# Two heads' values in one set of PSUM rows, value products divided by key tile, and last experts' sums by TensorE, in a four-layer decoder kernel

## The chip, the cores and the metric

The kernel runs on one core of one Trainium2 chip. The metric is the device time of one execution in microseconds (us). TensorE is called PE here, VectorE DVE, ScalarE ACT, GpSimd POOL and SyncE SP. Each runs its own queue of instructions in order, and they wait for one another by semaphores.

## The reference

The input x has 16 sequences of 256 tokens with 128 values each, and a context of 16 x 64 x 64. Four layers each do a self attention, a cross attention and a feed-forward part (dense or chosen experts), each added to x and layer-normalised. What matters for the change:

```python
# self attentions of layers 0 to 2, 16 heads of 8 values, 256 queries x 256 keys
scores = einsum('bhqd,bhkd->bhqk', q, k) * 8 ** -0.5     # + mask or bias
out    = einsum('bhqk,bhkd->bhqd', softmax(scores, -1), v)
# L0 self: rotary.  L0 cross: causal self attention + cross attention, added.
# L1 self: bias by distance, out * sigmoid(x @ Wgate.T + bgate).
# L2 self: additive mask, repeated three times, out of one is q of the next.
# L2 feed-forward: causal rotary attention, then capped experts.
# L3 feed-forward: each token's four chosen experts of 16
y = sum over 4 chosen of w[k] * expert_k(x);  x = layernorm(x + y)
```

## The kernel before

Everything but the experts' rows stays in SBUF. Stages follow one another; each of the later attentions begins its first slots inside the last slots of the stage ahead (`lead`).

`SelfAttention` is built five times: s0 (L0, rotary), s1 (L0 causal with cross attention), s3 (L1, bias and gate), s6 (L2, three repetitions), s8 (the attention of L2's feed-forward part, kind "keep"). A unit is one sequence (and one repetition): 16 units in each, 48 in s6, 112 in all. The work is written out by hand in slots: unit u starts 8 slots (10 in s1) after unit u-1, and in slot g every engine's `..._slot` issues what the offsets call for. In the first 8 slots of a unit PE makes plain scores of two heads a slot (L1314, with masks L1348) and DVE takes their maxima (L1359, L1362); at slot 8 `dve_neg_max` (L670) splits the negated maxima into two bf16 terms, with four instructions. From slot LE = 12 on PE makes transposed scores with the maxima subtracted (L1452), and ACT takes exponentials into PT (L1412, in s3 L1403 after DVE has added the bias at L1480).

Four times in a unit (j = 0 to 3, slots LE+3, 5, 7, 9) `pe_pv` (L1489) multiplies four heads' exponentials by their values: 9 columns a head (8 values and a one, whose product is the sum), each head in its own 32 PSUM rows of bank 6, all four at once. j = 0 and 1 fill the bank. ACT copies it to TV (`act_tv`, L718), PE transposes it with four fp32 transposes (`pe_tvt`, L727), and DVE takes reciprocals of the sums (L738) and multiplies twice (L744). j = 2 and 3 do all of this again. s1 has a third round for its cross attention (L754, L759). Then come the transpose of the unit's output (`pe_oot`, L767), the output projection (L348), residual, norm and the transpose for the next stage, at `OUT` and `TURN`. Reciprocal square roots of the norms are made by `newton` (L492), twelve small instructions on POOL.

The values of a chunk (two sequences) are projected by `pe_values` (L1263) and put in one of three buffers VA by ACT or DVE (L1277, L1285); for chunk 0 that is 13 to 19 slots before its first unit. PSUM bank 7 is shared in turn by all transposes and projections (`pj_take`).

The last stage, s12 (`ChosenExperts`, "marked"), runs blocks of expert rows. POOL scatters each block's results (`pool_result`, L3751), gathers the results of chunks 0 to 4 (`pool_gather`, L3763), and makes the root of the chunk before in between. The results of chunks 5 to 7 come by plain DMA, and `dve_results` (L3797) sums them on DVE (L3804, L3807), takes moments and normalises.

## Time and profile before

| | us |
|---|---|
| time, median of 3 runs | 4086.99 (4083.13 to 4093.6) |
| the profiled execution's own time | 4104.95 |
| its span | 4103.1 |
| granted PE clock, mean | 0.87 |
| PE busy | 3225.7 (79%) |
| DVE busy | 2729.5 (67%) |
| ACT busy | 2072.7 (51%) |
| POOL busy | 1254.2 (31%) |

A row of the groups has the line, engine, operation and tiles, the count, busy us and the mean ns of one, then idle time ahead of it. Stretches are given in us from the span's start. The five attentions lie at about 50 to 355 (s0), 373 to 760 (s1), 986 to 1374 (s3), 1869 to 2610 (s6) and 2807 to 3070 (s8); s12's blocks end at 4060.

### The profile page before, as it was taken

Reading aid. Unit: us, or ns where it says so; the run is one execution under the profiler, and the core shown is the slowest. Engines: PE = TensorE matmul, PEld = TensorE weight load, DVE = VectorE, ACT = ScalarE, POOL = GpSimd, SP = SyncE. Lnnn points to the kernel's source line nnn. Section 1 sums busy time; section 2 is a strip of 40 time slices with the busy share of each in tenths; the row PEclk is TensorE's granted clock in tenths of the full one; section 3 lists DMA queues with packets and bytes.
Section 4 is the critical chain, followed back from the end, with each engine's and each line's share of the span. In section 5 each row is a group of like instructions: output and inputs, shape, how many; then the busy total and the mean of one; then the engine's idle time right before and its main releaser. Section 6 shows DMA issues by size and latency. Waiting matters only on the chain.

```text
span 4103.1 us, 91932 instructions
## 1 busy us (share of the span) xinstructions
PE 3225.7 (79%) x33262; PEld 2229.8 (54%) x33262; DVE 2729.5 (67%) x7583; ACT 2072.7 (51%) x4651; POOL 1254.2 (31%) x2347
## 2 busy tenths in 40 slices
PE   6886888696888676967898989677883579879884
PEld 2443555473556455854555555344553456669884
DVE  5884767364778576547787878476766468865455
ACT  2664656322444453535787878453660234345563
POOL 2321222102121234451111111243322424534666
PEclk9987999697999787977999999687995599989997
DMA  5423332032221322231212121423412260122323
GB/s 92 69 38 55 59 54 39 21 100 40 37 39 18 57 60 66 85 72 38 47 30 45 29 43 31 59 39 60 60 32 71 72 112 21 50 85 85 94 75 92
DMA packets 322828, 232.76 MB, mean 57 GB/s; under 512 B 53901, under 2 KB 305531, under 8 KB 322199
## 3 DMA queue, kind: packets, MB, share of 16 engines
q1 hardware_dynamic: 308106, 198.55, 24.7%
q0 software_dynamic: 13408, 27.54, 2.2%
q8 instruction: 269, 4.41, 0.5%
q14 instruction: 181, 1.48, 0.1%
q10 hardware_dynamic: 864, 0.79, 0.1%
HBM read 69.28 MB, written 55.75 MB: 30 GB/s over the span
## 4 chain that ended last, share of the span: by engine, by line
PE 26%; DVE 13%; POOL 7%; issue 6%; ACT 4%; DMA 2%; SPq 1%; DVEq 0%; ACTq 0%; POOLq 0%
PE ps L1505 4%; PE ps L1314 3%; PE ps L3939 2%; PE ps L3948 2%; PE ps L1348 2%; POOL PT L3763 2%; PE ps L727 2%; PE ps L1452 2%; ACT PT L1412 1%; DVE M L1362 1%; POOL L_sorted_results L3751 1%; PE ps L1126 1%; DVE X L406 1%; DMA SKB<-MT 1%; DVE BS L378 1%
## 5 line engine op out<-in xcount | busy, mean ns | idle before, releaser
L1412 ACT ACTIVATE PT<-ps 128x512 f32<-128x512 f32 (+1 forms) x1600 | 812.0, 560 | 339.6 <-PE ps L1348 247.4
L1362 DVE TENSOR_REDUCE M<-ps 128x2 f32<-128x512 f32 x1024 | 652.6, 683 | 128.6 <-PE ps L1348 103.8
L1314 PE MATMUL ps<-SKB 51*128 51x256 bf16 (+3 forms) x3584 | 414.4, 276 | 115.7 <-DVE M L1362 66.2
L1359 DVE TENSOR_REDUCE M<-ps 128x3 f32<-128x384 f32 x768 | 390.6, 550 | 150.5 <-PE ps L1348 92.7
L1505 PE MATMUL ps<-PT,VA 128*9 128x256 f32 (+1 forms) x7168 | 455.7, 374 | 1.4 <-ACT PT L1412 1.2
L4021 ACT ACTIVATE SKB<-ps,SKB 128x128 f32<-128x128 f32 x1032 | 295.1, 370 | 242.4 <-PE ps L3939 241.0
L1452 PE MATMUL ps<-SKB 53*128 53x256 bf16 (+3 forms) x3584 | 357.8, 268 | 47.2 <-DMA SKB<-MT 37.3
L1348 PE MATMUL ps<-tri,idh 64*128 64x128 bf16 x5120 | 392.9, 222 | 0.0
L4091 DVE COPY SKB<-SKB 128x1028 f32 (+1 forms) x258 | 185.7, 720 | 259.7 <-PE ps L3948 232.4
L1314 PEld LDWEIGHTS ps<-SKB 51*128 51x128 bf16 (+1 forms) x3584 | 131.2, 96 | 385.9 <-DVE M L1362 158.1
L3948 PE MATMUL ps<-SKB 128*128 128x128 f32 x2064 | 286.6, 284 | 28.4 <-ACT SKB L4021 28.3
L649 POOL TENSOR_TENSOR FF<-FF,HH 128x512 f32<-128x512 f32 (+1 forms) x118 | 128.9, 1092 | 546.4 <-ACT HH L638 546.3
L1348 PEld LDWEIGHTS ps<-tri,idh 64*128 64x128 bf16 x5120 | 278.2, 98 | 28.0
L3939 PE MATMUL ps<-SKB 128*128 128x128 f32 x2064 | 290.7, 286 | 0.0
L3948 PEld LDWEIGHTS ps<-SKB 128*128 128x128 f32 x2064 | 263.4, 200 | 31.5 <-ACT SKB L4021 31.3
L3939 PEld LDWEIGHTS ps<-SKB 128*128 128x128 f32 x2064 | 267.5, 202 | 0.5 <-issue 0.3
L496 POOL TENSOR_TENSOR NW<-NW 128x4 f32<-128x4 f32 x336 | 70.6, 210 | 600.7 <-DVE NW L489 546.6
L1505 PEld LDWEIGHTS ps<-PT,VA 128*9 128x9 f32 x7168 | 156.4, 92 | 168.4 <-issue 40.1
L727 PE MATMUL ps<-idf,TV 128*128 128x128 f32 x1088 | 183.6, 294 | 51.6 <-ACT TV L718 17.8
L1452 PEld LDWEIGHTS ps<-SKB 53*128 53x128 bf16 (+1 forms) x3584 | 160.1, 97 | 84.5 <-DMA SKB<-MT 41.4
L3821 POOL DMA_INDIRECT L_sorted_rows<-XT,GG x144 | 145.7, 1012 | 188.8 <-DVE SKB L4098 79.1
L1403 ACT ACTIVATE PT<-ps 128x768 f32<-128x768 f32 x128 | 103.9, 811 | 185.9 <-DVE ps L1480 185.9
(520 smaller groups left out, 6403.3 us busy)
## 6 DMA issues: line engine op xcount, KB each, us to landing
SKB<-HH SPq DMA_DIRECT2D x1212, 64.0 KB
SKB<-HH SPq DMA_DIRECT2D x576, 32.0 KB
L_sorted_results<-SKB SPq DMA_DIRECT2D x195, 64.0 KB
PT<-L_sorted_rows SPq DMA_DIRECT2D x150, 64.0 KB
SKB<-in_L3f_w SPq DMA_DIRECT2D x32, 256.0 KB, 3.6
L_sorted_rows<-TV SPq DMA_DIRECT2D x2, 4032.0 KB, 32.4
SKB<-scratch SPq DMA_DIRECT2D x2, 2048.0 KB, 11.5
SKB<-in_L1f_w SPq DMA_DIRECT2D x16, 256.0 KB, 3.2
```

What stands on the lines that cost most here:

```text
L727: k = e.transpose(pj[:, 256 * qt + 128 * g:256 * qt + 128 * g + 128], K.TV[:, 256 * g + 128 * qt:256 * g + 128 * qt + 128], K.idf[:, :])
L1314: k = e.matmul(self.mx_bank(m + i)[:, o:o + n], K.QS[self.set(c)][64 * i:64 * i + rows, s, 256 * bb + 128 * qt:256 * bb + 128 * qt + 128], ...
L1348: return e.matmul(blocks[:, :, 64 * sub:64 * sub + 64], K.idh[sub][part, :], tri, start=False, stop=sub == 1)
L1359: k = e.tensor_reduce(K.M3[n % 2][:, hh, 0:3], mx[:, 0:384].rearrange("p (a k) -> p a k", a=3), axis=AX.X, op=ALU.max)
L1362: k = e.tensor_reduce(K.M3[n % 2][:, hh, 0:2], mx.rearrange("p (a k) -> p a k", a=2), axis=AX.X, op=ALU.max)
L1412: e.activation(K.PT[:, x % 4, n * i:n * i + n], self.st_bank(x, i)[:, 0:n], ACT.Exp, bias=0.0, scale=self.scale).then_inc(*self.exp.inc())
L1452: k = e.matmul(self.st_bank(x, i)[:, 256 * kt:512 - lo if kt else 256], k1, q1, start=kt == 0, stop=plain and kt == 1)
L1505: k = e.matmul(K.PS[32 * i:32 * i + 9, 6, 256 * g + lo:256 * g + 256], K.VA[self.set(c)][:, (2 * bb + kt) * 16 + 8 * (i % 2) + 2 * j + i / ...
L3939: k = e.matmul(K.PS[:, 2 + m % 2, 128 * hc:128 * hc + 128], self.WT[m % 3][:, 128 * hc:128 * hc + 128], self.XC[m % 3], start=True, stop=True)
L3948: k = e.matmul(K.PS[:, 4 + m % 2, 0:128], self.HB[m % 3][:, hc, :], self.WT[m % 3][:, 512 + 128 * hc:640 + 128 * hc], start=hc == 0, stop= ...
L4021: k = e.activation(self.HB[n % 3][:, hc, :], K.PS[:, 2 + n % 2, 128 * hc:128 * hc + 128], self.func, bias=self.WT[n % 3][:, 1024 + hc:1025 ...
L4091: e.tensor_copy(self.WT[n % 3], self.table[:, bass.ds(at, TC)]).then_inc(*self.wt.inc())
```

## The change

In the five self attentions the values of heads j and j+2 go to the same 32 PSUM rows: a weight of 18 columns has nine of values and nine of zeros, and j = 0 to 3 are accumulated. Bank 6 then holds the whole unit, so one copy, one set of four transposes and one normalising remain in place of two. In s0, s1 and s3 ACT copies the transposed values out of PSUM (`act_vn`), DVE takes the reciprocals from there and POOL multiplies; in s6 and s8 (`quick`) DVE does both from PSUM. In s0, s3 and s8 (`split`) the products with key tile 1 are issued one slot later, between the plain scores and the transposed scores. Maxima lie in another order (MX3), so that `dve_neg_max` has two instructions for them instead of four. VA has two buffers, and the values of a chunk are projected at another slot: 8 slots after its first unit's start at most. Output, out-projection and turn slots of s0, s1 and s3 lie later; s0 has 3 slots more at its end and s3 has 4. In s12 the roots of chunks 0 to 4 are made by DVE, and PE sums the results of chunks 5 to 7 by products with the identity.

```diff
-        self.VA = [sb(f"VA{i}", [128, 64, 9]) for i in range(3)]
+        self.VA = [sb(f"VA{i}", [128, 32, 27]) for i in range(2)]
@@ dve_neg_max
+        if order == "self":
+            e.tensor_scalar(o[:, :, 0, :], v, -1.0, None, ALU.mult).then_inc(*K.dv.inc())
+            e.wait_ge(*K.dv.now())
+            e.scalar_tensor_tensor(out=o[:, :, 1, :], in0=v, scalar=-1.0, in1=o[:, :, 0, :], op0=ALU.mult, op1=ALU.subtract
+                                   ).then_inc(*self.negmax.inc())
+            return
@@ new
+    def act_vn(self, e, f):
...
+        if f > 0:
+            e.wait_ge(*self.nrm.at(f - 1))
+        e.activation(self.VN, K.PS[:, 7, :].rearrange("p (x k) -> p x k", k=32)[:, :, 0:18], ACT.Copy, bias=0.0, scale=1.0
+                     ).then_inc(*self.vn.inc())
+    def pool_normalise(self, e, f, oo):
...
+        for h in range(2):
+            for half in range(2):
+                k = e.tensor_tensor(out[:, :, h, 4 * half:4 * half + 4, :], v[:, :, :, h, half, 0:8],
+                                    r[:, :, :, h, half:half + 1].to_broadcast([128, 2, 4, 8]), ALU.mult)
@@ SelfAttention
-    LE, MBT, CMBT, TV, GATE = 12, 9, 11, (5, 9, 11), 8
+    LE, MBT, CMBT, GATE = 12, 9, 11, 8
+    TV = (9, 11)
-        self.OOS = LE + (14 if cross else 12 if gate else 11)
-        self.OUT, self.TURN = self.OOS + 1, 6 if cross or gate else 5
+        self.quick, self.split = reps > 1 or kind == "keep", rope or gate
+        self.OOS = LE + (15 if cross else 11 if self.quick else 14)
+        self.OUT, self.TURN = (28, 5) if cross else (31, 8) if gate else (24, 5) if reps > 1 else (24, 8) if self.quick else (31, 6)
-        self.nf, self.nm = 2 + cross, 1 + cross
+        self.nf, self.nm = 1 + cross, 1 + cross
@@ pe_pv
-        for kt in range(2):
+        for kt in tiles:
...
-                k = e.matmul(K.PS[32 * i:32 * i + 9, 6, 256 * g + lo:256 * g + 256],
...
-                             start=kt == 0, stop=kt == 1)
+                k = e.matmul(K.PS[32 * i:32 * i + 18, 6, 256 * g + lo:256 * g + 256],
+                             K.VA[c % 2][:, pair, 9 * half:9 * half + 18], pt[:, i % 2, o:o + 256 - lo],
+                             start=j == 0 and kt == 0, stop=j == 3 and kt == 1)
@@ pe_slot, between pe_max_mask and pe_exp
+        for j in range(3):
+            u = self.at(g, LE + 2 * j + 4)
+            if u is not None and self.split:
+                self.pe_pv(e, u, j, (1,))
...
-                self.pe_pv(e, u, j)
+                self.pe_pv(e, u, j, (0,) if self.split and j < 3 else (0, 1))
@@ ChosenExperts.pool_gather
-        if k == top - 1 and c > 0:
-            self.tail.pool_root(e, c - 1)
@@ ChosenExperts, new
+    def pe_results(self, e, c):
+
+        K, total = self.K, self.total_of(c)
+        e.wait_ge(*self.x.at(c))
+        e.matmul(total, K.idf[:, :], K.xc(c), start=True, stop=False)
+        for t in (2 * c - 10, 2 * c - 9):
+            e.wait_ge(*self.results.at(t))
+        for k in range(self.top):
+            o = e.matmul(total, K.idf[:, :], self.results_of(c)[:, :, k, :], start=False, stop=k == self.top - 1)
+        o.then_inc(*self.total.inc())
@@ dve_results
-            o = e.tensor_reduce(total[:, j, :], self.YY[t].rearrange("p k d -> p d k"), axis=AX.X, op=ALU.add)
...
-        e.tensor_tensor(K.xc(c), K.xc(c), total, ALU.add).then_inc(*self.total.inc())
         e.wait_ge(*self.total.at(c - 5))
-        self.tail.dve_moments(e, c)
+        self.tail.dve_moments(e, c, self.total_of(c))
@@ dve_sum
+        if self.marked and c > 0 and k < 2:
+            (self.tail.dve_root, self.tail.dve_norm)[k](e, c - 1)
```

## Rows read from the trace of the kernel before

**Rows 1.** The page's first two parts: busy us, and granted clock in 40 slices.
```profile
PE 3225.7 (79%) x33262; PEld 2229.8 (54%) x33262; DVE 2729.5 (67%) x7583; ACT 2072.7 (51%) x4651; POOL 1254.2 (31%) x2347
PEclk9987999697999787977999999687995599989997
```

**Rows 2.** Busy time by stretch (stretch, its length, busy and count of each engine, clock).
```profile
100.00:340.00 240.00, 200.58 (x2090) 97.69 (x2090) 199.84 (x524) 162.60 (x305) 64.32 (x124) 0.91 0.34 52
1050.00:1350.00 300.00, 256.67 (x2884) 175.98 (x2884) 234.91 (x613) 129.47 (x209) 54.05 (x123) 0.95 0.20 29
1910.00:2560.00 650.00, 580.43 (x9188) 362.33 (x9183) 537.73 (x1274) 502.49 (x995) 92.53 (x167) 0.98 0.20 37
```

**Rows 3.** Waits in 1910 to 2560, of PE and of DVE (us, times, longest).
```profile
PE ps L1314 <- DVE M L1362: 38.8, 83, 1.8
DVE M L1362 <- PE ps L1348: 93.5, 124, 5.0
```

**Rows 4.** Timeline of s6, one round of transposing and normalising (start, us, engine, line).
```profile
2151.39 0.63 PE L727 MATMUL ps<-idf,TV 128*128 128x128 f32 x4
2151.95 0.39 PE L1314 MATMUL ps<-SKB 51*128 51x256 bf16 x4
2152.26 0.25 DVE L738 RECIPROCAL RC<-ps 128x16 f32<-128x16 f32 x1
2152.54 0.41 DVE L744 TENSOR_TENSOR OO<-ps,RC 128x64 f32<-128x64 f32 x2
```

**Rows 5.** Timeline of s6, the first of the four instructions of `dve_neg_max`.
```profile
2155.89 0.16 DVE L683 TENSOR_SCALAR MB<-M 128x16 bf16<-128x16 f32 x1
```

**Rows 6.** Timeline of PE: a value block and what follows it; a block of s1's cross values.
```profile
2159.57 1.05 PE L1505 MATMUL ps<-PT,VA 128*9 128x256 f32 x16
2160.56 0.39 PE L1314 MATMUL ps<-SKB 51*128 51x256 bf16 x4
...
580.93 0.63 PE L1433 MATMUL ps<-PT,SKB 128*18 128x256 f32 x8
```

**Rows 7.** Groups by line and shape: two sizes of two-input operations on POOL.
```profile
L1548 POOL TENSOR_TENSOR OO<-OO,OC 128x256 f32<-128x256 f32 x32 | 23.3, 727 | 219.3 <-DVE OC L1539 138.5 <-DVE OC L759 80.8
L498 POOL TENSOR_TENSOR NW<-NW 128x4 f32<-128x4 f32 x336 | 69.6, 207 | 26.4
```

**Rows 8.** Timeline: a chunk's value projection in s0's full slots.
```profile
206.25 1.16 PE L1263 MATMUL ps<-WB,XT 128*128 128x128 f32 x8
```

**Rows 9.** Timeline of s3's last unit: copy of the values, and the output's transpose.
```profile
1371.30 0.60 ACT L718 ACTIVATE TV<-ps 128x512 f32<-128x512 f32 x1 [0.96 <-PE ps L1505]
...
1374.57 0.66 PE L767 MATMUL ps<-idf,OO 128*128 128x128 f32 x2 [1.90 <-POOL OO L1548]
```

**Rows 10.** s12's last blocks by stretch (as rows 2); POOL's timeline, first and last instruction of a root.
```profile
3935.00:4068.00 133.00, 99.84 (x797) 97.40 (x796) 62.28 (x180) 67.92 (x242) 102.95 (x128) 0.91 0.25 67
...
4060.95 0.21 POOL L496 TENSOR_TENSOR NW<-NW 128x4 f32<-128x4 f32 x1
...
4064.10 0.20 POOL L502 TENSOR_TENSOR RSD<-NW 128x4 f32<-128x4 f32 x1
```

**Rows 11.** Timeline of DVE at the end: first sum of chunk 5, last add of chunk 7.
```profile
4074.03 1.94 DVE L3804 TENSOR_REDUCE FF<-XT 128x128 f32<-128x512 f32 x2 [7.91 <-DMA XT<-L_sorted_results]
...
4093.18 0.69 DVE L3807 TENSOR_TENSOR X<-X,FF 128x512 f32<-128x512 f32 x1
```

**Rows 12.** Clock before the last sums; one fp32 product of 512 columns at either clock.
```profile
4064.00:4074.00 10.00, 0.00 (x0) 0.00 (x0) 1.92 (x12) 0.00 (x0) 6.56 (x18) 0.50 0.31 93
...
201.70 1.12 PE L1126 MATMUL ps<-XT,WB 128*128 128x512 f32 x2
...
2611.21 2.07 PE L2095 MATMUL ps<-XT,WB 128*128 128x512 f32 x2 [0.47 <-ACT OT L777]
```

**Rows 13.** Timeline of s0: a wait of PE and the transposes behind it.
```profile
216.51 0.39 PE L1314 MATMUL ps<-SKB 48*128 48x256 bf16 x3 [2.04 <-DVE M L1362]
...
217.25 1.11 PE L727 MATMUL ps<-idf,TV 128*128 128x128 f32 x4
```

More of the change, by code:

```diff
@@ L373, in norm, with dve_moments @@
         return 2 * c + second if self.kind == "rms" else c
-    def dve_moments(self, e, c):
-        K, n, rr = self.K, self.norm(c), self.rows(c)
+    def dve_moments(self, e, c, source=None):
+        K, n, rr = self.K, self.norm(c), self.rows(c) if source is None else source
         for i in range(4):
@@ new lines, in dve_recip @@
+    def dve_recip(self, e, f):
+        K = self.K
+        e.wait_ge(*self.vn.at(f))
+        sums = self.VN.rearrange("p x (e k) -> p x e k", e=2)[:, :, :, 8]
+        e.reciprocal(K.RC[f % 2][:, 0:32].rearrange("p (x e) -> p x e", e=2), sums).then_inc(*self.rc.inc())
+    def pool_normalise(self, e, f, oo):
+        K = self.K
+        v = self.VN.rearrange("p (q b h) (e k) -> p q b h e k", q=2, h=2, e=2)
+        r = K.RC[f % 2][:, 0:32].rearrange("p (q b h e) -> p q b h e", q=2, h=2, e=2)
+        out = oo.rearrange("p q (h d b) -> p q h b d", h=2, d=8)
+        e.wait_ge(*self.rc.at(f))
+        for h in range(2):
+            for half in range(2):
+                k = e.tensor_tensor(out[:, :, h, 4 * half:4 * half + 4, :], v[:, :, :, h, half, 0:8],
+                                    r[:, :, :, h, half:half + 1].to_broadcast([128, 2, 4, 8]), ALU.mult)
+        return k
@@ new lines, in pool_normalise_cross @@
+    def pool_normalise_cross(self, e, f, oo):
+        K = self.K
+        v = self.VN.rearrange("p (q b) (h k) -> p q b h k", q=2, h=2)
+        r = K.RC[f % 2][:, 0:32].rearrange("p (q b h) -> p q b h", q=2, h=2)
+        out = oo.rearrange("p q (h d b) -> p q h b d", h=2, d=8)
+        e.wait_ge(*self.rc.at(f))
+        for h in range(2):
+            k = e.tensor_tensor(out[:, :, h, :, :], v[:, :, :, h, 0:8],
+                                r[:, :, :, h:h + 1].to_broadcast([128, 2, 8, 8]), ALU.mult)
@@ L1276, in act_values @@
         self.values_free(e, c)
-        e.activation(K.VA[self.set(c)][:, :, 0:8], K.PS[:, 7, :].rearrange("p (a k) -> p a k", k=8), ACT.Copy, bias=0.0,
-                     scale=1.0).then_inc(*self.vact.inc())
+        v = K.PS[:, 7, :].rearrange("p (x e b k) -> p x e b k", e=2, b=4, k=8)
+        va = K.VA[c % 2][:, :, :].rearrange("p (x b) k -> p x b k", b=4)
+        for half in range(2):
+            k = e.activation(va[:, :, :, 18 * half:18 * half + 8], v[:, :, half, :, :], ACT.Copy, bias=0.0, scale=1.0)
+        k.then_inc(*self.vact.inc())
     def dve_values(self, e, c):
@@ L1720, in act_slot @@
             self.act_mt(e, self.nm * u)
+        for h, off in enumerate(self.TV):
+            u = self.at(g, LE + off + 1)
+            if u is not None and h < self.nf and not self.quick:
+                self.act_vn(e, self.nf * u + h)
         u = self.at(g, self.CMBT)
@@ L1772, in dve_slot @@
             self.dve_neg_max(e, 2 * u + 1, "cross")
-        for h, off in ((0, LE + 6), (1, LE + 10), (2, LE + 12)):
-            u = self.at(g, off)
-            if u is not None and h < self.nf:
-                self.dve_norm(e, u, h)
+        for h, off in enumerate(self.TV):
+            u = self.at(g, LE + off + 2)
+            if u is not None and h < self.nf and not self.quick:
+                self.dve_recip(e, self.nf * u + h)
+        u = self.at(g, LE + self.TV[0] + 1)
+        if u is not None and self.quick:
+            self.dve_norm(e, u)
         u = self.at(g, LE + self.GATE)
@@ L1799, in pool_slot @@
             self.begin.all_in(e)
+        for h, off in enumerate(self.TV):
+            u = self.at(g, LE + off + 2)
+            if u is not None and h < self.nf and not self.quick:
+                self.pool_norm(e, u, h)
         u = self.at(g, self.OOS - 1)
@@ L3959, in pe @@
                 self.pe_b2(e, c)
+        if self.marked:
+            for c in (5, 6, 7):
+                self.pe_results(e, c)
         if not self.last:
@@ L4061, in dve_sum @@
             self.tail.dve_moments(e, c)
-            if c > 0:
+            if c > 0 and not self.marked:
                 self.tail.dve_norm(e, c - 1)
```

182 lines of the change are left out of this document (99 added, 83 removed).

## The prediction

> **What bounds the kernel now.** I read the page's first two parts first. PE is busy 79% of the span, DVE 67%, and PE's clock is near its upper level in most slices [rows 1]. An average over stages says little, so I next took busy time by stretch, in the full part of three of the five attentions [rows 2]. In s0 PE and DVE are busy 84% and 83% (200.58 and 199.84 of 240), in s3 86% and 78%, in s6 89% and 83%. ACT stands at 68%, 43% and 77%, POOL at 27% or less. So no engine alone sets the pace; PE does most, with DVE close behind. The waits show how the two are tied: in s6 PE's plain scores wait for DVE's maxima 83 times (38.8 us), and DVE's maxima wait for PE's masks 124 times (93.5 us) [rows 3]. With three PSUM banks for maxima neither can run more than a slot and a half ahead. A gain must therefore come off both. In a slot with much extra PE work DVE waits, in a slot without it PE waits.
>
> In the last stage's last 133 us POOL is the bound: it is busy 102.95 us with 128 instructions [rows 10], and its timeline shows a hole of only 0.30 us behind each indirect DMA (92 of the 128, 28 us). A root is a piece of twelve small instructions in that chain [rows 10]. At the very end DVE sums alone [rows 11].
>
> **The change part by part.** All sums are made against the profiled execution (4104.95 us); it is 18 us above the median of the runs, and I take the 18 us off at the end.
>
> *One round of transposing less, PE.* Each of the 112 units loses four fp32 transposes. From their start to the start of the next scores is 2151.95 - 2151.39 = 0.56 us [rows 4]. 112 x 0.56 = 63 us of PE's queue.
>
> *The same on DVE.* A round is a reciprocal of 0.25 us and a pair of multiplications of 0.41 us [rows 4]. Of the four instructions of the negated maxima, at 0.16 us [rows 5], two go. In s6 and s8 one reciprocal goes and the four multiplications stay: 0.25 + 0.32 = 0.57 us a unit. In s0, s1 and s3 the multiplications go to POOL too: 0.57 + 0.82 = 1.4 us a unit.
>
> *What that is worth.* In the 64 units of s6 and s8 PE sheds 0.56 and DVE 0.57 us, so both sides of the ring get shorter by the same and I count 0.56: 36 us. In s1, where PE has the cross attention besides, I count PE's part and a little: 0.7 x 16 = 11 us. In s0 and s3 DVE is as near the bound as PE and sheds 1.4 us; I take the middle of 0.56 and 1.4, 1.0 us: 32 units, 32 us. Together 79 us. The low end is half of it (40 us), where an engine that does not shed in the right slot takes up the rest. The high end is 1.0 us for each unit (112 us).
>
> *POOL and ACT.* POOL gets four multiplications of 128x64 a unit. No row shows that size; between 207 ns for 4 columns and 727 ns for 256 [rows 7] a straight line gives 207 + 60 x 2.06 = 331 ns, so 1.3 us a unit with bounds 0.8 and 2.9 us, on an engine that is idle at least 73% of these stretches [rows 2]. Nothing behind them on POOL is due within a unit: I cost it at nothing. If that cover were gone, `act_vn` of the next round would wait for POOL and hold ACT's exponentials behind it; that is the end for s1, whose two rounds are two slots apart, at most 1 us x 16 units = 16 us. ACT loses a copy of 512 columns a unit and in three attentions gains one of 288: nothing.
>
> *Eighteen columns of weights.* The cross block of s1 has them: 8 instructions take 0.63 us, 16 with nine columns take 1.05 us [rows 6]. With 0.21 us for every four, both are so many rounds plus 0.21 us at the end. So 18 columns cost nothing; 0.02 us a block (448 blocks, 9 us) is the most the rows leave.
>
> *Products divided by key tile.* In s0, s3 and s8 three of the four blocks of a unit are cut in two: 144 cuts. Two blocks of 8 take 2 x 0.63 = 1.26 us against 1.05 us, so a cut costs up to 0.21 us, 30 us in all. Against it, half a block in each slot in place of a whole one in every second evens out PE's slots, and with them the waits of both sides. In s6, whose waits I read, DVE waits 93.5 us for PE in some 44 units, about 2 us a unit; a fifth of that in 48 units would be 20 us. I take the two as equal: 0, from -20 to +30 us.
>
> The Trainium skill, in TensorEngine Tiling (Array Packing), Key Properties, says that a change of tiling mode drains TensorE; here the scores use row tiles and the values column tiles, so each cut adds a change there and back. By that rule the cut costs its full price. The trace bears out the size of a block's end, but it shows the next scores starting 0.06 us before the block is over. This rule has its case among the rivals.
>
> *Values projected later.* Chunk 0's values used to be projected ahead of the first unit, where PE has idle time. Now they lie in full slots, 1.16 us of PE [rows 8], once in each attention: 5 us lost, from 0 to 10. The buffers' waits are met, since the last products of the chunk two before lie ahead.
>
> *Ends of the attentions.* In s3's last unit, from the copy of the values to the output's transpose 3.3 us pass [rows 9], and everything waits for this chain. In s0, s1 and s3 it gets a second copy (288 columns; 512 take 0.60 us [rows 9], and I take 0.45), and four multiplications on POOL in place of two on DVE (+0.9 us), with a handover more: some 1.7 us each, 5 us, and 1 us for the extra empty slots of s0 and s3. 6 us lost, from 3 to 15.
>
> *The last stage.* Roots of chunks 1 to 3 lie in the stretch where POOL is the bound; each takes 4064.30 - 4060.95 = 3.35 us [rows 10]: 10 us gained. On DVE, at half load there, they are hidden; what would be late next is a block's row copy, by 2.5 us once a chunk. For chunk 0's root, made before that stretch, I count nothing. The sums of chunks 5 to 7 take from 4074.03 to 4093.87, 19.8 us, with moments and norms in between [rows 11]. PE does them as 4 + 5 + 5 products of 512 columns. One takes 1.12 us at 2.4 GHz and 2.07 us at 1.2 GHz [rows 12]; back to back I count 0.88 and 1.75 us, since the end of one overlaps the next. The granted clock is 0.50 just before [rows 12], so they begin at 1.2 GHz: 14 products are 12.3 us at full and 24.5 us at half clock. I take 4 us at the lower level and the rest at the upper: 4 + 11.7 x 0.88 = 14.3 us, and 5 us gained, from -5 to +7. Moments, root and norm of chunk 7 stay behind. Together 15 us gained.
>
> **The sum.** 79 + 0 + 0 - 5 - 6 + 15 = 83 us. 4105 - 83 = 4022 us for a profiled execution, 4087 - 83 = 4004 us for the median.
>
> **The rivals.**
>
> *A. Half of it is taken up.* The ring between PE and DVE is worked in slots. When the transposes leave their slot, the next scores find the maxima's banks not yet free, and PE waits for DVE instead. For it: PE already waits 38.8 us there [rows 3]. Against it: DVE sheds as much. 79 becomes 40 us: 4043 us.
>
> *B. The cuts cost their full price,* 30 us (by the rule above, the trace agrees only in part): 4034 us.
>
> *C. It all comes off, and the evened slots help.* 1.0 us for each unit (112 us) and 10 us from the cuts: 4087 - 112 - 10 - 4 = 3961 us.
>
> *D. Slower: the clock.* After a wait of 2.04 us in s0, four transposes take 1.11 us in place of 0.63 [rows 13, 4]: PE had dropped to 1.2 GHz. If PE, with less to do, drops more often, its work slows. The attentions last some 1900 us; a mean granted clock 0.04 lower costs 76 us and eats nearly the whole gain, and 0.06 lower gives 4087 - 83 + 114 = 4118 us. It decides from about 0.045 on. Against it: the period gets shorter with the work, so PE's share hardly falls.
>
> *E. It does not do what it says:* the removed rounds were covered by waits already, and ends, cuts and later projections take what is left: 4080 us.
>
> **How the numbers follow.** Forecast 0.45, A 0.18, B 0.12, C 0.14, D 0.06, E 0.05. The forecast's own range is 3985 to 4022. The range over the cases runs from 3955 (C with its spread) to 4060 (A with the low ends of ends and cuts); D, E and the far part of C are left out. A measurement of this kernel can tell about 0.3% (12 us) from no change. Faster by more than that: 0.45 + 0.18 + 0.12 + 0.14 = 0.89. Within it: E, 0.05. Slower: D, 0.06.
>
> **What would show it.** The transposes' group (L727 before) falls from 1088 to 640; the copies to TV from 272 to 160. Right: s6 shorter by some 27 us, with PE's waits for the maxima no longer than now; s0 and s3 by 16 us each; about 10 us less between the first and last scatter of results in s12; the last sums on PE from about 4 us into them at the upper clock. A shows as PE's waits for maxima grown by 20 us or more in s6. B shows as value blocks of 8 that take 0.63 us in s3 and s8 while neither engine's waits fall. D shows in the granted clock of the stretches. Wrong would be a stage that gets longer, above all s1, by ACT's second copy waiting for POOL, or transitions longer by over 3 us.

## The result and the profile after

The changed kernel takes 4061.92 us (median of 6 runs, 4055.12 to 4065.14), the kernel before 4095.56 us beside it. The ratio is 0.9926, with a 95% interval of 0.9909 to 0.9943: faster by 0.7%, some 34 us by the two medians, where 83 us were forecast. The profiled execution took 4061.09 us, its span is 4059.1 us.

The page's first two parts, of after (they answer to [rows 1]):

```profile
PE 3212.7 (79%) x32844; PEld 2171.8 (54%) x32844; DVE 2651.9 (65%) x7053; ACT 2045.4 (50%) x4611; POOL 1307.1 (32%) x2511
PEclk9986999697999778977999999687995589989998
```

PE's busy time fell by 13 us only, although 448 transposes are gone: the cut value products take 86.7, 65.9 and 66.3 us in s0, s3 and s8, where they took 75.4, 56.4 and 55.4, some 32 us more. Groups by line and shape, of after: the transposes, the copies to TV, POOL's new multiplications and the first of the two instructions of the negated maxima.

```profile
L741 PE MATMUL ps<-idf,TV 128*128 128x128 f32 x640 | 108.1, 294 | 25.6 <-ACT TV L732 16.4 <-ACT XT L468 2.4 <-DVE SKB L991 1.5
L732 ACT ACTIVATE TV<-ps 128x512 f32<-128x512 f32 x160 | 95.6, 597 | 19.5 <-PE ps L1569 11.2 <-PE ps L2232 7.9 <-PE ps L1495 0.2
L786 POOL TENSOR_TENSOR OO<-GG,RC 128x64 f32<-128x64 f32 x128 | 35.6, 315 | 173.8 <-DVE RC L775 173.8
L688 DVE TENSOR_SCALAR MB<-M 128x32 bf16<-128x32 f32 x112 | 30.5, 272 | 0.3
```

The counts are those forecast (640, 160), so the change does what it says. POOL's multiplication takes 0.315 us where 0.331 was estimated. In s6 an instruction of the negated maxima takes 0.17 us at twice the size (0.16 before), so two of them save half of four; over all attentions the mean of one is 272 ns in place of 189, and the saving is smaller.

Busy time by stretch, of after (as [rows 2]; the stages lie up to 24 us earlier):

```profile
100.00:340.00 240.00, 209.07 (x2038) 84.44 (x2035) 186.19 (x415) 157.78 (x307) 77.35 (x168) 0.88 0.34 51
1050.00:1350.00 300.00, 262.08 (x2865) 165.48 (x2860) 224.21 (x522) 132.59 (x218) 74.84 (x187) 0.95 0.23 32
1910.00:2560.00 650.00, 566.57 (x8920) 351.89 (x8917) 520.84 (x1141) 481.27 (x942) 95.31 (x178) 0.96 0.18 37
```

In s0 DVE sheds 14 us and PE, with fewer instructions, is busy 8 us longer: its value products are cut there, and the granted clock is 0.88 where it was 0.91. Waits of PE and DVE in 1910 to 2560, of after (as [rows 3], with the wait of the transposed scores for the shift's DMA):

```profile
DVE M L1424 <- PE ps L1410: 117.6, 181, 6.8
PE ps L1376 <- DVE M L1424: 45.9, 106, 1.5
PE ps L1514 <- DMA SKB<-MT: 30.2, 11, 6.6
```

Both sides wait more than before (93.5 and 38.8 us), and the third row is new in size: before it was 13.8 us in 3 waits.

Where the time went, by stage: from the first plain scores to the last value product, in us. Stages that an experiment left alone repeat the same work, so each stage has up to ten profiles of its changed form (two of its old one); they show how far one profile can be trusted. s1 has no cuts, so the three kernels without cuts repeat it too: 366.8, 366.7 and 363.3 us, outside the range of the ten. A stage of a single profile is good to some 5 us, no better.

| | before (two profiles) | after | mean of ten profiles with the changed form | forecast gain | gain |
|---|---|---|---|---|---|
| s0 | 302.3, 298.9 | 300.6 | 298.7 (296.3 to 300.6) | 16 | 2 |
| s1 | 382.6, 382.2 | 367.6 | 370.3 (367.6 to 374.0) | 11 | 12 |
| s3 | 384.5, 379.0 | 371.8 | 371.7 (369.9 to 373.6) | 16 | 10 |
| s6 | 735.9 | 740.7 | | 27 | -5 |
| s8 | 258.7, 257.6 | 261.5 | 256.9 (254.2 to 261.5) | 9 | 1 |

Of the stretches between, s0 to s1, s1 to s3 and s3 to s6 got longer by 0.6, 2.2 and 2.6 us, and s6 to s8 shorter by 7.4. From s8's end to the end of the span the two profiled runs take 1037.2 and 1017.2 us, but a second profile with the old code there (experiment 5) gives 1026.5, and 8 of the 20 us between the first two lie ahead of the first scatter of results, where the second old profile has none of them (842.4 us from s8's end in before, 831.4 in experiment 5, 833.9 in after). From the first scatter on, after gains 12 us, as shown below. Together 20 (attentions) + 7 - 5 + 12 = 34 us, the 34 measured; that it comes out so closely is partly chance, since each term is good to some us.

### The profile page after: what moved, and what is told of

Read it like the earlier page. It is cut to its first block, busy times and chain, and to the rows that moved or that the text cites. A ratio compares the mean times of both kernels' runs of the same rounds, so it can differ in the third digit from the quotient of the medians.

```text
span 4059.1 us, 90396 instructions
## 1 busy us (share of the span) xinstructions
PE 3212.7 (79%) x32844; PEld 2171.8 (54%) x32844; DVE 2651.9 (65%) x7053; ACT 2045.4 (50%) x4611; POOL 1307.1 (32%) x2511
## 4 chain that ended last, share of the span: by engine, by line
PE 27%; DVE 14%; POOL 6%; issue 5%; SPq 3%; DMA 3%; ACT 2%; DVEq 0%; POOLq 0%; ACTq 0%
PE ps L1569 5%; PE ps L1376 3%; PE ps L4030 2%; PE ps L4039 2%; SPq L676 2%; PE ps L1410 2%; DVE M L1424 2%; PE ps L1514 2%; POOL PT L3845 2%; DMA SKB<-MT 1%; POOL L_sorted_results L3833 1%; PE ps L1184 1%; DVE X L414 1%; DVE BS L381 1%; PE ps L741 1%
## 5 line engine op out<-in xcount | busy, mean ns | idle before, releaser
L1376 PE MATMUL ps<-SKB 51*128 51x256 bf16 (+3 forms) x3584 | 426.0, 278 | 139.7 <-DVE M L1424 71.9
L1569 PE MATMUL ps<-PT,VA 128*18 128x256 f32 (+1 forms) x7168 | 492.7, 382 | 0.0
L1569 PEld LDWEIGHTS ps<-PT,VA 128*18 128x18 f32 x7168 | 157.0, 99 | 155.7 <-issue 54.4
L1514 PEld LDWEIGHTS ps<-SKB 53*128 53x128 bf16 (+1 forms) x3584 | 147.7, 97 | 169.4 <-DMA SKB<-MT 60.9
L1184 PE MATMUL ps<-XT,WB 128*128 128x512 f32 x224 | 154.9, 780 | 42.4 <-ACT FF L1200 14.0
```

Of the source, the lines that this page charges most:

```text
L1184: k = e.matmul(pj, W[f"{kind}{part}"], K.xt(key), start=True, stop=True)
L1376: k = e.matmul(self.mx_bank(m + i)[:, o:o + n], K.QS[self.set(c)][64 * i:64 * i + rows, s, 256 * bb + 128 * qt:256 * bb + 128 * qt + 128], ...
L1514: k = e.matmul(self.st_bank(x, i)[:, 256 * kt:512 - lo if kt else 256], k1, q1, start=kt == 0, stop=plain and kt == 1)
L1569: k = e.matmul(K.PS[32 * i:32 * i + 18, 6, 256 * g + lo:256 * g + 256], K.VA[c % 2][:, pair, 9 * half:9 * half + 18], pt[:, i % 2, o:o + 2 ...
```

## The experiments

Spans and ratios alone can't separate effects of 5 us here (a ratio has an interval of some 0.2% to each side, 8 us), so most verdicts rest on the length of one stage and on the unit's period, from one transpose of the output to the next, which repeats to 0.01 us in s6's steady units: 13.08 us before, 12.87 after. Experiments 4, 7 to 10 and both kernels of 14 ran once each (4069.2, 4043.1, 4047.2, 4027.9, 4061.9, 4031.8 and 4068.4 us), so they have no ratio.

**1. No cuts.** `self.split` is False in every attention.

```diff
-        self.quick, self.split = reps > 1 or kind == "keep", rope or gate
+        self.quick, self.split = reps > 1 or kind == "keep", False
```

> The changed kernel, but with the value products whole in all attentions (no cuts). Theory (the cuts cost their price, rival B): value products' busy time falls by about 10 us in each of s0, s3 and s8 (66.3 to about 56 us in s8), and each of these stages gets shorter by 6 to 10 us: s0 300.6 to about 292, s3 371.8 to about 364, s8 261.5 to about 253; the whole 20 to 28 us faster than the changed kernel, about 0.986 of the kernel before. Rival (the cuts pay for themselves by evening the slots): the busy time falls the same, but waits of PE for the maxima and of DVE for PE grow, and the three stages stay within 3 us or get longer; the whole at 0.992 to 1.0. s1 and s6 stay at 367.6 and 740.7 by both.

4049.31 us, ratio 0.9903 (0.9876 to 0.9931). s0 292.5 (at a granted clock of 0.93), s3 368.4, s8 255.5. Neither theory was borne out in full; experiments 6 and 13 repeat it.

**2. Shifts issued by ACT.** In s6 the two DMAs of `sp_self_shift` leave SP's queue.

```diff
             self.act_mt(e, self.nm * u)
+            if self.reps > 1:
...
+                self.sp_self_shift(e, u)
```

> The changed kernel, but s6's two shift DMAs of a unit are issued by ACT right behind its copy to MT instead of by SP. Theory (s6 lost its gain to SP's queue, which issues a DMA each 0.67 us in order, 14 a unit): PE's waits of the transposed scores for SKB<-MT fall from 30 us to under 8, and s6 gets shorter by 15 to 25 us, 740.7 to about 720. Rival 1 (the stacks' DMAs land late too, so the transposed or plain scores wait for them next): the wait for SKB<-HH grows by as much, s6 shorter by less than 5. Rival 2 (ACT has no time for the issue): ACT's exponentials fall behind, s6 longer by 48 times the issue's time, some 5 to 30 us.

4075.7 us, ratio 0.9973 (0.9954 to 0.9992); s6 757.4 us, 17 longer. Rival 2. ACT's timeline in s6:

```profile
1938.82 0.37 ACT L717 ACTIVATE MT<-ps 32x256 bf16<-32x256 bf16 x1
1939.22 1.37 ACTq L1306 DMA_DIRECT2D SKB<-MT  x2
1940.69 2.28 ACT L1477 ACTIVATE PT<-ps 128x512 f32<-128x512 f32 x4 [1.50 <-issue]
```

Two issues take ACT 1.37 us. PE's waits for the shift did fall (30.2 to 12.5 us), but PE then waited 37.9 us in 47 places for exponentials, where it had waited 2.0, and the steady unit grew from 12.87 to 13.89 us. ACT was busy 74% and had seemed to have room; it has none at that place.

**3. The old slots for q and k in s6.** The change moves the projections of q and k one and two slots later and k's stacks by one. My prediction doesn't mention these edits.

```diff
-        self.Q, self.KP, self.V = ... else (-24, -13, 4)
+        self.Q, self.KP, self.V = ... else (-25, -15, 4) if reps > 1 else (-24, -13, 4)
-        self.QSTK, self.KSTK = (-26, -17) if cross else (-20, -11) if reps > 1 else ...
+        self.QSTK, self.KSTK = (-26, -17) if cross else (-20, -12) if reps > 1 else ...
```

> The changed kernel, but in s6 alone the projections and the stacks of q and k lie in the slots of the kernel before (Q -25, KP -15, KSTK -12 in place of -24, -13, -11). Theory (K's stacks, one slot later, push SP's shifts behind them): the long waits of the transposed scores for SKB<-MT return to about 3 to 5 in place of 11 (30 us to about 14), and s6 gets shorter by 10 to 16 us, to about 727. Rival (the queue is full whatever the slots; only the shorter unit, 12.87 in place of 13.08 us, overruns it): s6 stays within 4 us of 740.7 with 8 or more such waits.

4035.31 us, ratio 0.9873 (0.9849 to 0.9897); s6 718.0 us, shorter by 22.7; the waits for the shift are 15.8 us in 6. SP's timeline, of after and then of this kernel:

```profile
2020.87 0.64 SPq L1303 DMA_DIRECT2D SKB<-MT  x1
2029.45 9.51 SPq L676 DMA_DIRECT2D SKB<-HH  x12
2039.01 18.85 SPq L1303 DMA_DIRECT2D SKB<-MT  x4
```

```profile
2023.12 8.52 SPq L676 DMA_DIRECT2D SKB<-HH  x12
2035.48 14.64 SPq L1303 DMA_DIRECT2D SKB<-MT  x4
```

And PE's timeline, of after:

```profile
2044.71 0.39 PE L1514 MATMUL ps<-SKB 53*128 53x256 bf16 x4 [3.21 <-DMA SKB<-MT]
```

In after SP stands still from 2021.5 to 2029.45 with k's stack at the head of its queue, whose source isn't ready (SP waits 7.9 us for ACT's write of HH); the twelve DMAs then take 9.51 us, and the shift behind them goes out at 2039.01 and holds PE for 3.21 us. With the old slots the stack goes out 6.3 us earlier, and this wait is gone.

**4. PE's saving put back.** Four transposes of the identity, which nobody waits for, in the slot of the removed round in s6.

```diff
+        if self.at(g, LE + 6) is not None and self.reps > 1:
+            pj = self.turns_take(e)
+            for i in range(4):
+                e.transpose(pj[:, 128 * i:128 * i + 128], K.idf[:, :], K.idf[:, :])
```

> The changed kernel, but in each of s6's 48 units PE makes four fp32 transposes of the identity in the slot where the removed round was (nothing waits for them). Theory (rival A: the slot was waiting for the maxima anyway): the steady unit goes from 12.87 to at most 13.1 us (+0.2), PE's waits for DVE's maxima fall from 47.7 us back to about 39, s6 longer by 5 to 12 us. Rival (the round's 0.56 us was paid in full and something else in the change ate the gain): the unit goes to 13.4 us, s6 longer by 25 us or more.

The steady unit goes from 12.87 to 12.94 us and PE's waits for the maxima from 48.8 to 33.7 us; s6 747.2. On PE the removed 0.56 us were worth 0.07. That s6 grew by 6.5 us and not by 48 x 0.07 = 3 goes with the waits for the shift, which went from 30.2 to 37.9 us.

**5. The new slots in the kernel before.** The reverse of 3, with nothing else of the change.

```diff
-        self.Q, self.KP, self.V = ... else (-25, -15, -19)
+        self.Q, self.KP, self.V = ... else (-24, -13, -19) if reps > 1 else (-25, -15, -19)
-        self.QSTK, self.KSTK = (-26, -17) if cross else (-20, -12) if reps > 1 else ...
+        self.QSTK, self.KSTK = (-26, -17) if cross else (-20, -11) if reps > 1 else ...
```

> The kernel before, with nothing of the change but s6's slots for the projections and stacks of q and k (Q -24, KP -13, KSTK -11 in place of -25, -15, -12). Theory (the later K stacks hold SP's queue, and the shifts behind them come late, whatever else the kernel does): the transposed scores' waits for SKB<-MT go from 3 (14 us) to 8 or more (over 25 us), s6 from 735.9 to 750 to 760 us, the whole 12 to 25 us slower than before, ratio 1.003 to 1.006. Rival (the kernel before had slack there, and only the changed kernel's shorter unit makes the stacks late): s6 within 5 us of 735.9, ratio within 0.998 to 1.002.

4114.12 us, ratio 1.0065 (1.0045 to 1.0085); 10 waits for the shift (27.4 us), s6 746.1, longer by 10. The slots cost time without the rest of the change too. How much is less sure: the ratio says 27 us for the whole, and the execution with the profile (4092.07 us) was the fastest of five, so 10 us in s6 may be low.

**6. Both: old slots and no cuts,** the edits of 1 and 3 together.

> The changed kernel with both: s6's old slots for q and k (as in e3_old_slots) and no cuts in any attention (as in e1_nosplit). If the two act in different stages and add: s0 about 292, s3 about 368, s6 about 718, s8 about 255; 9 to 12 us faster than e3_old_slots, ratio to the kernel before about 0.985. Rival (the cuts' gain was the chance of one profile; it ran 4049 in place of 4062): s0 and s3 stay at 299 and 371 and the ratio at 0.987 to 0.988.

4037.28 us, ratio 0.9863 (0.9843 to 0.9883). s0 300.3, s3 374.0, s6 716.5, s8 252.0. The short s0 of experiment 1 did not come again; the granted clock in s0 is 0.89 here and was 0.93 there.

**7 and 8. Maxima shortened, and both savings put back.** On top of 3, in s6: 7 takes the maxima of slot 3 over half the keys; 8 puts back the transposes of experiment 4 and three small operations of DVE.

```diff
+                if self.reps > 1 and s == 3:
+                    v = v[:, :, 0:128]
```

> As e3_old_slots, but in one slot of each unit of s6 the two maxima are taken over the first 128 keys of 256 (it leaves out half of that slot's maxima), which takes some 0.54 us off DVE in a unit and nothing off PE. Theory (the steady unit is now paced by DVE through the maxima's banks): the unit falls from 12.87 by 0.3 to 0.54 us and s6 by 15 to 25 us. Rival 1 (PE's work is the bound again): the unit falls by less than 0.1. Rival 2 (the ring's handovers are the bound, either side's shortening is half used): 0.1 to 0.3.

```diff
+        if self.at(g, LE + 6) is not None and self.reps > 1:
+            for i in range(3):
+                e.tensor_scalar(K.OV[:, 256:272], K.idf[:, 0:16], -1.0, None, ALU.mult).then_inc(*K.dv.inc())
+                e.wait_ge(*K.dv.now())
```

> As e3_old_slots, but in each unit of s6 both savings are put back as dead work in the slot of the removed round: four fp32 transposes on PE and three small operations on DVE (some 0.5 us). Theory (the two savings are what made the unit shorter; PE's alone was worth 0.07): the unit returns to 13.0 to 13.15 us and s6 to 725 to 732. Rival (the unit's time comes from something else in the change, such as the one-piece normalising or the 18 columns): the unit goes well past 13.2 or stays at 12.95.

With 7 the unit stays at 12.87 us and s6 at 720.0: 0.54 us less on DVE bring nothing. With 8 the unit is 12.94 and s6 724.6, so in the steady unit DVE's part adds nothing to PE's 0.07. Neither engine's sum sets the unit. The rows of experiment 3's kernel show what does, in PE's timeline and then in DVE's:

```profile
1916.89 0.27 PE L1376 MATMUL ps<-SKB 51*128 51x256 bf16 x1
1917.50 0.39 PE L1376 MATMUL ps<-SKB 51*128 51x256 bf16 x3 [0.34 <-DVE M L1424]
...
1918.26 1.06 PE L1569 MATMUL ps<-PT,VA 128*18 128x256 f32 x16
1919.26 0.39 PE L1376 MATMUL ps<-SKB 51*128 51x256 bf16 x4
```

```profile
1916.75 2.53 DVE L1424 TENSOR_REDUCE M<-ps 128x2 f32<-128x512 f32 x4 [0.34 <-PE ps L1410]
1919.80 2.53 DVE L1424 TENSOR_REDUCE M<-ps 128x2 f32<-128x512 f32 x4 [0.51 <-PE ps L1410]
```

PE stops at the second head's plain scores until the first of DVE's four maxima has freed its bank (1916.75 + 0.63 = 1917.38). It then makes the rest, the transposed scores and the value block, and only then the next plain scores, for which DVE waits until 1919.80. 0.63 + 2.42 = 3.05 us is one turn of this ring, a pair of slots. Both engines wait once in such a turn. Work outside the ring (the other three maxima, and what PE does in the slot without a value block) costs nothing as long as it fits into the waits.

A unit has four turns. Measured from one start of plain scores behind a value block to the next, as medians over the steady units, in us:

| | turn 1 | turn 2 | turn 3 | turn 4 | unit |
|---|---|---|---|---|---|
| before | 3.20 | 3.29 | 3.04 | 3.56 | 13.08 |
| experiment 3 | 3.21 | 3.05 | 3.05 | 3.57 | 12.87 |
| experiments 4 and 8 | 3.21 | 3.12 | 3.05 | 3.57 | 12.94 |
| experiment 9 | 3.21 | 2.95 | 2.95 | 3.57 | 12.68 |
| experiment 11 | 3.38 | 3.29 | 3.29 | 3.66 | 13.61 |

Turn 4 has the remaining transposes; there PE does not wait for the maxima at all, and its own work sets the turn. Turn 2 had the removed round. It is the only turn that got shorter, from 3.29 to the 3.05 of a turn without a round. The dead transposes bring back 0.07 of these 0.24. The rest can be read from the rows of turn 2, of before and then of experiment 8:

```profile
1938.97 0.39 PE L1314 MATMUL ps<-SKB 51*128 51x256 bf16 x4
1939.01 0.60 ACT L718 ACTIVATE TV<-ps 128x512 f32<-128x512 f32 x1
1939.51 0.36 ACT L703 ACTIVATE MT<-ps 32x256 bf16<-32x256 bf16 x1
1939.91 0.42 PEld L727 LDWEIGHTS ps<-idf,TV 128*128 128x128 f32 x4 [0.28 <-ACT MT L703]
```

```profile
1914.85 0.39 PE L1376 MATMUL ps<-SKB 51*128 51x256 bf16 x4
1914.96 0.37 ACT L717 ACTIVATE MT<-ps 32x256 bf16<-32x256 bf16 x1
1915.62 0.42 PEld L1747 LDWEIGHTS ps<-idf 128*128 128x128 f32 x4
```

(PEld is PE's weight load.) The transposes use the shared bank 7, which ACT must first empty by its copy to MT. Before, ACT's copy to TV stood ahead of that one, so the transposes began 0.94 us behind the scores in place of 0.77: 0.17 us, which is 3.29 - 3.12. So most of the gain in the steady unit came from ACT's removed copy. This is read from rows; no run put that copy back.

**9. The same saving inside the ring.** As 7, but for the first head in slots 2 and 4.

```diff
+                if self.reps > 1 and s in (2, 4) and i == 0:
+                    v = v[:, :, 0:128]
```

> As e3_old_slots, but in two slots of each unit of s6 (slots 2 and 4) the maxima of the first head alone are taken over 128 keys of 256 (it leaves out half of these two maxima): again 0.54 us off DVE in a unit, as in e7_short_maxima, where it brought nothing. Theory (the unit is set by a ring: the first maxima of an even slot, then PE's second plain scores of the odd slot, its transposed scores, its value block of 1.06 us and the first plain scores of the next slot; only work inside that ring counts): these two maxima lie in the ring, and the unit falls from 12.87 to 12.35 to 12.6 us, s6 by 12 to 25 us. Rival (DVE's time has nothing to do with the unit at all, as e7 suggests): 12.87 stays.

The unit falls to 12.68 us, s6 to 713.6. The place of the 0.54 us decides whether it counts, as the ring says; but only 0.19 of it came, less than the range given. PE's waits, of experiment 9, with those of its weight loads, and one of these in the timeline:

```profile
PE ps L1376 <- DVE M L1427: 21.9, 43, 1.5
PEld ps L1517 <- ACT PT L1477: 21.9, 92, 1.1
PE ps L1517 <- ACT PT L1477: 5.2, 11, 0.9
...
1948.24 0.11 PEld L1517 LDWEIGHTS ps<-SKB 53*128 53x128 bf16 x4 [0.17 <-ACT PT L1477]
```

The weight loads of the transposed scores wait for ACT's exponentials in 92 places, where they did in 12 (7.0 us) in experiment 3.

**10 and 11. Cuts in s6, and another order.** 10 cuts the value products in s6 too. 11 issues the transposed scores ahead of the plain ones in slots with a value block.

```diff
@@ 10
-        self.quick, self.split = reps > 1 or kind == "keep", rope or gate
+        self.quick, self.split = reps > 1 or kind == "keep", rope or gate or reps > 1
@@ 11
+        turned = scores and self.reps > 1 and any(self.at(g, LE + 2 * j + 3) is not None for j in range(4))
+        if turned:
+            self.pe_exp(e, *scores)
+            self.pe_exp_mask(e, *scores)
         if maxima:
             self.pe_max(e, *maxima)
...
-        if scores:
+        if scores and not turned:
             self.pe_exp(e, *scores)
...
```

> As e3_old_slots, but with the value products cut by key tile in s6 too. By the ring, half of the block leaves it for the even slot (0.5 us shorter in each pair of slots), but three cuts of 0.21 us come on top of PE, which has some 1.0 us of waits in a unit: the unit goes to 12.6 to 12.9 us, s6 within -12 and +3 of e3's 718. Rival (a cut is only a cost): the unit goes to 13.1 or more, s6 longer by 10 us or more.

> As e3_old_slots, but in those slots of s6 that have a value block PE issues the transposed scores and their masks ahead of the plain ones (same work, another order). Theory (ring): the transposed scores (some 0.45 us) leave the ring in every pair of slots, PE and DVE are then bound by their own sums (PE 11.9, DVE 12.3 us a unit): the unit falls from 12.87 to 12.3 to 12.6 us, s6 from 718 to 695 to 708, the whole 10 to 23 us faster than e3_old_slots, ratio to the kernel before 0.982 to 0.985. Rival (the ring is only a way of writing down what PE's and DVE's sums do): the unit and the ratio (0.987) stay.

Both rivals won on the time: 10 has a unit of 13.46 us and s6 748.3, 11 has 13.61 and 750.8 (4073.44 us, ratio 0.9956, 0.9938 to 0.9974). Waits of PE, of experiment 10 and then of 11:

```profile
PE ps L1514 <- ACT PT L1474: 43.3, 118, 0.9
PE ps L1376 <- DVE M L1424: 5.2, 3, 1.8
```

```profile
PE ps L1514 <- ACT PT L1474: 87.8, 126, 1.1
PE ps L1376 <- DVE M L1424: 4.4, 3, 1.5
```

The waits for the maxima are gone, as the ring through DVE says (49.5 to 4.4 us), and a second ring took over, through the exponentials' banks and ACT: 5.1 us of waits in experiment 3, 87.8 here. The two lie close together; by the weight loads' waits above, that is also why 9 gained a third only.

**12. The other order everywhere,** without cuts: 11 without its `self.reps > 1`, on top of 6.

> As e6_slots_nosplit (old slots in s6, no cuts anywhere), with the order of e11_order_s6 in all five attentions. Theory (ring): with no cuts each stage has whole value blocks in every second slot, so the same ring binds it and s0, s3 and s8 get shorter by 3 to 8 us each beside s6's 10 to 23; ratio to the kernel before 0.976 to 0.983. Rival (s0 and s3 are bound by DVE's or PE's sum, with rotary and bias work in between): these stages stay within 3 us of 292, 368 and 255 and the ratio is that of e11_order_s6.

4077.57 us, ratio 0.9964 (0.9946 to 0.9981); s3 384.9, longer by 13, s6 751.1, s0 297.9 and s8 255.7. No gain in any stage.

**13. Stacks spread, with and without cuts.** In s6 the twelve DMAs of a stack go out over six slots in place of three, on top of 3; the second kernel has no cuts besides.

```diff
-        self.stack_slots = 3 if reps > 1 else 6
+        self.stack_slots = 6
```

> As e3_old_slots, but in s6 the twelve stack DMAs of q and of k are issued over six slots, two at a time, in place of three slots, four at a time. Theory (the remaining long waits for SKB<-MT, 3 to 6 of 4 to 6 us, come of the 26 DMAs that SP issues in one row between two shifts): the shift finds its turn in between, waits for SKB<-MT fall from 16 us to under 6, s6 from 718 to 705 to 713, ratio to the kernel before 0.984 to 0.986. Rival (k's stacks then land after the first unit's start and its plain scores wait for them instead): waits for SKB<-HH grow by as much, s6 within 5 us of 718 or longer.

> As e13_spread_stacks (s6's old slots, stacks over six slots), and no cuts in any attention. If the cuts cost their PE time where PE sets the stage (s8, as e14_pe_back showed): s8 250 to 253 in place of 257, s0 and s3 within 3 us of 298.6 and 371.7, since DVE sets those; ratio to the kernel before 0.984 to 0.987. If the cuts cost in s0 and s3 too: s0 about 292, s3 about 366, ratio 0.982 to 0.985. If they cost nothing anywhere: all three stages as with cuts, ratio 0.987 to 0.989.

The first: 4036.64 us, 0.9878 (0.9853 to 0.9903); s6 716.0, the waits for the shift 10.0 us in 4. They fell as expected, but s6 gained 2 us only. The second: 4021.99 us, 0.9822 (0.9803 to 0.9841), the best of all: s0 300.8, s3 368.4, s6 716.6, s8 252.0.

**14. Each engine's saving put back in the other stages.** On top of 3, in s0, s1, s3 and s8: one kernel has the dead transposes of experiment 4, the other dead operations of DVE, 1.42 us for seven in s0, s1 and s3, and three in s8.

```diff
+        if self.at(g, LE + 6) is not None and self.reps == 1:
+            for i in range(3 if self.quick else 7):
+                e.tensor_scalar(K.M3[0][:, 12:16, :], K.idf[:, 0:16].rearrange("p (a b) -> p a b", a=4), -1.0, None, ALU.mult
...
```

> As e3_old_slots, but in the slot of the removed round of every unit of s0, s1, s3 and s8 PE makes four fp32 transposes of the identity (0.56 us). Unchanged, these stages last 298.6 (from 296.3 to 300.6 in nine runs), 370, 371.7 and 257 us. Theory 1 (PE sets these stages, so the saving was real and the cuts and the rest ate it): s0, s3 and s8 get longer by 7 to 11 us each. Theory 2 (the saving lies outside what binds, as in s6, 0.07 us a unit): each stays within 3 us.

> As e3_old_slots, but in the slot of the removed round of every unit DVE makes seven small operations in s0, s1 and s3 (some 1.4 us) and three in s8 (some 0.6 us). Theory 1 (DVE sets s0 and s3 as much as PE): s0 and s3 get longer by 8 to 16 us each, s8 by 3 to 8. Theory 2 (DVE's time outside the ring is worth nothing, as e7_short_maxima showed for s6): all stay within 3 us of 298.6, 370, 371.7 and 257.

| us | s0 | s1 | s3 | s8 |
|---|---|---|---|---|
| mean of ten | 298.7 | 370.3 | 371.7 | 256.9 |
| PE's saving back | 298.3 | 367.5 | 365.0 | 264.4 |
| DVE's saving back | 305.9 | 390.0 | 381.0 | 255.9 |

In s8 PE sets the stage: its pairs of units go from 14.4 + 17.0 to 14.8 + 17.35 us, 0.4 a unit. In s0, s1 and s3 it is DVE: s1 pays 20 us of the 23 put back, s3 9 and s0 7. There PE's round is worth nothing. These are single profiles; s1's 20 us and s3's 9 lie well outside the scatter, s0's 7 lies 5 above the longest of the ten.

## Why the prediction was wrong

It lies 58 us under the measured time, just outside its range of 3955 to 4060 us. Of these, 9 are the kernel before itself, whose median is 4095.6 us beside the result and was 4087.0 in the forecast. The other 49 are gain that did not come. By its own steps:

*Attentions' rounds, 79 us: failed, worth 20 as measured* (with the cuts and the later projections, which lie in the same stages). Of the 59 missing, 23 are the first of two things and 36 the rest. With the slots undone the attentions would give 43 us, which is the 40 of rival A.

First, **an edit was left out of the sum.** The step on what is moved speaks of values and output, not of q's and k's projections and k's stacks in s6, though a stack sits in SP's in-order queue ahead of the shifts and waits there for what the projection makes. The three slot numbers together cost 22.7 us by experiment 3, and 10 us alone by experiment 5. Without it s6 gains 736 - 718 = 18 us of the 27 forecast.

Second, **"both sides shed, so both sides gain" is the wrong step.** It read two busy shares and two rows of waits as a ring and then priced the ring by either engine's sum. In s6 PE's 0.56 us are worth 0.07 (experiment 4), and DVE's 0.54 us nothing or 0.19, by where they lie (7, 9). This is rival A, although not by its sign, PE's waits grown by 20 us or more: they grew by 7 [rows 3]. DVE's grew by 24, but 15 of these go with the slots (102.4 us in experiment 3). The period fell by 0.21, all of it in the turn that lost the round: 0.07 for PE's transposes and, by the rows, 0.17 for ACT's copy to TV, which the prediction put at nothing (the other three turns lost 0.03 together). 48 x 0.21 = 10 of s6's 18 us; the other 8 lie in the units where a chunk changes, and no experiment took them apart. In the other stages one engine sets the pace and only its part counts: DVE's in s1, s3 and s0, PE's in s8. s1's forecast, 11 us from PE's part, met the 12 measured by luck: PE's part is worth nothing there and DVE's 20, of which 8 did not come, and why stays open. In s8 PE's saving of 7 us was real and 1 was left; the cuts took 4 and the other 2 are within the scatter.

*Cuts, 0 (-20 to +30): within its bounds.* Value products' busy time in s8, experiment 13 with cuts and then without:

```profile
2754.80:3010.80 256.00, 63.95 (x1024) 19.29 (x1024) 0.94 0.33 54
2749.60:3001.70 252.10, 55.49 (x1024) 24.04 (x1024) 0.94 0.35 55
```

The first columns are the stretch, its length and PE's busy time in these products. 8.5 us for 48 cuts, 0.18 us each: rival B's full price (0.21) on PE, nearly. Its sign, blocks of 8 that take 0.63 us, is met by the halves with key tile 0; those with key tile 1 have 128 columns in s3 and s8 and take 0.41, a whole block 0.85 there. The Trainium skill's rule (TensorEngine Tiling (Array Packing), Key Properties), that a change of tiling mode drains the engine, thus agrees with the rows as far as PE's busy time goes. In stage lengths, three kernels without cuts give 297.9, 370.3 and 253.2 us as means against 298.7, 371.7 and 256.9: 4 us in s8, where PE sets the pace, and nothing that can be told from the scatter in s0 and s3. The two ratios with and without cuts disagree (0.9873 to 0.9863, 0.9878 to 0.9822), so the cuts' whole price is between nothing and some 20 us, most likely about 6. What they give in return, evened slots, shows on one side only in s8: PE's waits for the maxima are 11.8 us with cuts and 17.8 without, but DVE's for the masks 24.4 and 20.2. In s3 both are the same to some 3 us.

*s0, 16 forecast, 2 measured:* DVE's part is worth 7 by experiment 14, so 5 are missing. The granted clock is 0.91 and 0.93 in the two profiles of the old s0 and 0.88 to 0.90 in the ten of the new one; 0.03 of 300 us is 9 us of PE's work and would cover them. Kernels with the same s0 point the same way: without cuts it took 292.5 us at 0.93 and 300.3 and 300.8 at 0.89, in the old form 298.9 at 0.93 and 302.3 at 0.91. That is rival D in a small way, but no run set the clock, so it is not shown; with PE's dead work put back the clock was 0.91 and the stage still 298.3.

*Eighteen columns, 0: right.* A block takes 1.06 us, before 1.05 [rows 6]. *POOL, 0: right* by the 0.315 us of one multiplication; s1 did not get longer. *Values projected later, 5 us lost:* no run takes this term apart.

*Ends, 6 us lost: right in size.* The three transitions grew by 5.4 us. The chain of s3's last unit, timeline of after (as [rows 9]):

```profile
1344.50 0.60 ACT L732 ACTIVATE TV<-ps 128x512 f32<-128x512 f32 x1 [1.56 <-PE ps L1569]
...
1345.91 0.41 ACT L752 ACTIVATE GG<-ps 128x288 f32<-128x288 f32 x1 [0.50 <-PE ps L741]
1346.35 0.35 DVE L775 RECIPROCAL RC<-GG 128x32 f32<-128x32 f32 x1 [0.62 <-ACT GG L752]
...
1346.85 1.11 POOL L786 TENSOR_TENSOR OO<-GG,RC 128x64 f32<-128x64 f32 x4 [7.88 <-DVE RC L775]
...
1348.91 0.41 PE L821 MATMUL ps<-idf,OO 128*128 128x128 f32 x2 [1.88 <-POOL OO L1613]
```

From the copy to the transpose of the output 4.4 us pass in place of 3.3: 1.1 us more, 1.7 were forecast. If s0 and s1 pay the same, that is 3.3 of the 5.4 us; the empty slots are one candidate for the rest, which is not shown. *s6 to s8* became 7.4 us shorter, which nothing forecast and no experiment took apart.

*The last stage, 15 us: nearly right, about 12.* The scatters of results run from 3875.8 to 4026.6 in after, 150.8 us against 160.1: 9.3 gained of 10. This repeats well: the sixteen profiles with the new last stage have 148.2 to 150.8, the two with the old one 160.1 and 160.0. From the last scatter to the end it is 32.5 us against 34.8. The last sums, in PE's timeline, and then two stretches around them:

```profile
4034.83 6.12 PE L3888 MATMUL ps<-XT,idf 128*128 128x512 f32 x8 [13.43 <-DMA XT<-L_sorted_results]
...
4045.94 3.60 PE L3888 MATMUL ps<-PT,idf 128*128 128x512 f32 x8
```

```profile
4034.80:4041.00 6.20, 6.17 (x9) 2.75 (x10) 0.01 (x1) 0.00 (x0) 0.00 (x0) 0.60 1.05 368
4041.00:4050.00 9.00, 8.53 (x20) 3.42 (x18) 5.25 (x29) 0.00 (x0) 4.30 (x22) 1.00 0.35 105
```

They take 4049.54 - 4034.83 = 14.7 us (forecast 14.3, DVE took 19.8). A mean clock of 0.60 over 6.2 us is 5 us at the lower level (1.2 GHz) and the rest at the upper one (forecast: 4). But they begin 8.3 us behind the last scatter, DVE's began 5.7 behind it, so 2 to 3 of the 5 us remain.

## What to carry to other kernels

Where two engines hand buffers to each other and both wait, price an edit by its place in the cycle of waits, not by either engine's sum: the same 0.54 us was worth nothing outside it and 0.19 inside, and opening one ring brought up the next, through a third engine. Cut the period into turns and compare them one by one: here all of the gain lay in one turn of four, and most of it was a third engine's copy that had held a shared bank. Where one engine does set a stage, dead work put back on each engine in turn names it in two runs.

List every slot number that a change touches and follow each through the in-order queue of the DMAs. Projections and stacks issued one or two slots later cost more in s6 than the removed round of transposes gained there, and taking them back alone makes the kernel faster by 1.3% in place of 0.7%; with spread stacks and no cuts it is 1.8%.

## What the runs showed of the hardware

An issue of a small DMA (8 to 64 KB) holds its queue for 0.67 us on SP (1.34 for two; twelve in a row 7.9) and 0.69 us on ACT (1.37 for two), behind which ACT's next activation waited. A queue with 14 of them in a 12.87 us unit is 73% full by issue alone (14 x 0.67 = 9.4 us). The Trainium skill, in DMA: Bandwidth & Descriptors (Anatomy of one DMA — SWDGE (gpsimd) path), puts a sequencer's dispatch at some 50 ns and descriptor generation at "small, variable". That is the path of DMAs that GpSimd issues; these are issued by SP and ACT, so the figure doesn't price them, and no run here shows it.

In s3 the one kernel with PE's dead transposes ran at a granted clock of 0.95 and in 365.0 us, where ten others had 0.91 to 0.93 and 370 to 374: more work for PE and a shorter stage. It is one profile, and what the clock followed there stays open.
